# Destination one-hots one chunk later, and sums on three and four blocks of 32 TensorE columns, in a three-layer GCN behind an equivariant message layer

## The chip, the cores and the metric

The kernel runs on one core of a Trainium2 chip. The metric is the device time of one execution in microseconds (us). Of the kernel before, three executions took 5819.27, 5819.81 and 5830.06 us; the median is 5819.81.

## What is computed

There are 12500 nodes with 32 features and 200000 edges, sorted by destination. After a layer norm, a first part (layer 0) sends tensor-product messages along the edges. After a second layer norm come three graph convolutions with self loops and symmetric normalisation. They are what this change touches:

```
norm = deg_inv_sqrt[src] * deg_inv_sqrt[dst]
def conv(x, W, b):                 # W1: 32x128, W2: 128x128, W3: 128x32
    h = x @ W
    msg = h[src] * norm[:, None]
    return segment_sum(msg, dst) + b
h = relu(conv(x, W1, b1)); h = relu(conv(h, W2, b2)); h = relu(conv(h, W3, b3))
return x + h
```

The kernel sums before it multiplies by W1 and after it multiplies by W3, so the rows that it sums over the edges are 32 wide in layers 1 and 3 and 128 wide in layer 2 (WIDTH = [32, 32, 128, 32]).

## The kernel before

**Accumulator.** accT in SBUF holds features on partitions and nodes on the free axis: 12544 columns of nodes and 128 of margin. In layers 1 and 3 it uses partitions 0 to 31 (w = 32), in layer 2 all 128. Partition 32 holds the root of the degree in layer 1, to carry the bias as a 33rd row in the product with W1 (line 1764).

**Two ways over the edges.** Since the edges are sorted by destination, a stretch of edges falls into a narrow window of nodes. The first part of them is done in *groups* of 1024 edges: SP loads the source indices (line 490), POOL gathers the rows of the sources from a table in HBM with 8 indirect DMAs into `rows`, which has 4 buffers (line 641), ACT makes a one-hot of the destinations (lines 699 and 705), TensorE sums the group in `gathered_sum` with 8 fp32 products, rows by one-hot, into `sums` (line 1717; two matmul instructions for each product), and VectorE adds the window of 128 nodes to accT (line 1410, semaphore `added`). POOL may reuse a buffer of `rows` when the group four before has been added.

The rest is done in *buckets* of 1280 edges without a gather: `places` holds for each bucket which source row sits where. A bucket is cut into 5 *chunks*. For a chunk, `mark_sources` makes a one-hot of the sources (VectorE line 1298 in layers 2 and 3, ACT lines 796 and 805 in layer 1), `take` picks the rows from a table in SBUF with 20 products on four blocks of 32 TensorE columns (line 1648), ACT copies the result (`copy_bucket`, line 818), `mark_destinations` makes the one-hot of the destinations (VectorE, line 1313), and `give` sums over them with 5 products into psT or psX by turns (line 1662). After 5 chunks VectorE adds the bucket to accT (`add_bucket`, line 1373). The one-hots and the taken rows are double buffered by chunk.

Layer 1 has 120 groups and 61 buckets, layer 2 has 108 and 71, layer 3 has 80 and 93. Each layer is a loop; a pass has 4, 12 and 8 groups and 2, 8 and 10 buckets. Layer 1 also ranks the edges of later buckets (VectorE lines 1235 to 1280).

**Order.** The order on each engine is written by hand. For chunk k TensorE does `take(k)`, then a group's sum if one falls there, then `give(k - 1)`. VectorE does

```
mark_sources(n, step, k + 1)           # n > 1
...                                    # the group's add, if one falls on k
mark_destinations(n, step, k + 1)      # waits for give(k - 1)
if k % NCK == 0: add_bucket(...)       # the bucket that ended with chunk k - 1
```

In front of layer 3, in `table_after_second`, accT is multiplied by W2 and then by W3 (lines 1777 and 1785); POOL's gathers then start when the new table lies in HBM. At the end TensorE turns accT into blocks of nodes (line 1812), VectorE finishes each of 7 blocks with three instructions (lines 1484 to 1487), and SP stores them.

Of the kernel before, what the change touches and what calls it, by code (L numbers as in the profile page):

```python
# [70 lines left out]
KB = 25  # L71
KC = 5
# [36 lines left out]
def gnn_kernel(nc, x, src, dst, edge_attr, edge_weight, w1, b1, w2, b2,  # L109
               W1, B1, W2, B2, W3, B3, out):  # L110
    ctx = ExitStack()
    with ctx:
# [121 lines left out]
        W1s = sb("W1s", [F + 1, HID])  # L234
# [215 lines left out]
        def _(sp):  # L450
# [134 lines left out]
            sp.dma_start(accT[F:F + 1, 0:NPAD], accT[MUL:MUL + 1, 0:NPAD]).then_inc(counts_moved, 16)  # L585
# [20 lines left out]
        def _(pool):  # L606
# [20 lines left out]
            def gathers(n):  # L627
                def body(step, first, last):
# [15 lines left out]
                    if n == 0 and first:  # L644
# [19 lines left out]
        def _(act):  # L664
# [7 lines left out]
            act.dma_start(W1s[F:F + 1, :], B1.rearrange("(a n) -> a n", a=1)).then_inc(convs_in, 16)  # L672
# [77 lines left out]
            def own_term(n, rows_):  # L750

                for c, at, w in chunks:
# [11 lines left out]
            nc.scalar.activation(accT[F:F + 1, 0:NPAD], accT[F:F + 1, 0:NPAD], ACT.Sqrt,  # L764
                                 bias=one[F:F + 1, :]).then_inc(row_rooted, 1)
# [116 lines left out]
            act.wait_ge(convs_in, 96)  # L882
# [12 lines left out]
        def _(dve):  # L895
# [301 lines left out]
            def prepare_buckets():  # L1197
# [8 lines left out]
                                     iota[:, 0:BJ].unsqueeze(1).to_broadcast([P, BJ, BJ]), ALU.is_gt))  # L1206
                dve.wait_ge(start_b_moved, 32)
# [156 lines left out]
            def add_bucket(n, step, v_, u):  # L1364

                w = WIDTH[n]
# [6 lines left out]
                v.tensor_tensor(accT[0:w, window], accT[0:w, window], (psX if v_ % 2 else psT)[0:w, 0:BWIN],  # L1373
                                ALU.add).then_inc(bucket_added, 1)

            def conv(n):
                w = WIDTH[n]
# [13 lines left out]
                def body(step, first, last):  # L1391
                    groups, chunks_, starts_at = shape(n, last)
                    u = -1
                    for k in range(chunks_):
                        more = not (last and k == chunks_ - 1)
                        if more and n > 1:
                            mark_sources(n, step, k + 1)
                        if k in starts_at:
# [7 lines left out]
                            v_done = (k - 1) // NCK - 1  # L1406
# [18 lines left out]
                mark_destinations(n, Step(dve, 0, n), 0)  # L1425
# [53 lines left out]
            dve.wait_ge(convs_in, 96)  # L1479
# [356 lines left out]
```

## Time and profile before

| | |
|---|---|
| median of three executions | 5819.81 us |
| the profiled execution: its time, and its span | 5822.97 us, 5820.7 us |
| layer 0, and what follows it | 0 to 2280, to 2340 us |
| layer 1, and the product with W1 | 2340 to 3567, to 3626 us |
| layer 2, and the products with W2 and W3 | 3626 to 4739, to 4849 us |
| layer 3, and the output | 4849 to 5803, to 5821 us |
| TensorE, VectorE, ACT, POOL busy | 87%, 73%, 59%, 67% of the span |

The profile is of one execution. Engines are PE (TensorE; PEld is its weight loads), DVE (VectorE), ACT (ScalarE), POOL (GpSimd) and SP. A fp32 product shows as two matmul instructions. The last block of layer 0 is turned at 2288 us.

### The profile page before, as it was taken

How to read it: one execution, taken by the hardware profiler on the slowest of the kernel's cores; microseconds unless marked ns; L12 is line 12 of the kernel's file. 1: busy time of each engine (PE TensorE's matmuls, PEld its weight loads, DVE VectorE, ACT ScalarE, POOL GpSimd, SP SyncE). 2: the span in 40 equal slices, each digit the busy share in tenths (PEclk: the TensorE clock that was granted, in tenths of full speed). 3: DMA queues.
4: the chain of work that ended last, by engine and by line, in shares of the span. 5: the costliest groups of instructions: out<-in, count | busy, mean ns of one | idle time of the engine just before them, and what ended most of it. 6: DMA issues, size and time to landing. Idle time of an engine off the chain costs nothing.

```text
span 5820.7 us, 188939 instructions
## 1 busy us (share of the span) xinstructions
PE 5063.7 (87%) x70625; PEld 3798.9 (65%) x70626; DVE 4230.4 (73%) x8656; ACT 3414.6 (59%) x7724; POOL 3925.4 (67%) x4051
## 2 busy tenths in 40 slices
PE   2999999999999998576766678999999998888887
PEld 1555555555555554566656667988888977777777
DVE  5999999999999998677777775444444434665655
ACT  3666666666666664777777775555555534444434
POOL 4777777777777772677777774777777735665655
PEclk9999999999999999889898888999999988999999
DMA  5111111111111113111111112333333332222222
GB/s 68 39 36 36 36 36 37 36 36 36 36 36 37 36 36 35 34 34 36 34 34 34 35 35 74 83 81 80 81 83 80 79 91 46 56 58 54 58 52 53
DMA packets 474532, 290.23 MB, mean 50 GB/s; under 512 B 264732, under 2 KB 446784, under 8 KB 473393
## 3 DMA queue, kind: packets, MB, share of 16 engines
q0 software_dynamic: 129024, 108.79, 10.0%
q1 hardware_dynamic: 224524, 73.86, 6.3%
q10 hardware_dynamic: 120356, 98.86, 5.7%
q8 instruction: 437, 7.16, 0.5%
q14 instruction: 191, 1.56, 0.1%
HBM read 267.86 MB, written 13.27 MB: 48 GB/s over the span
## 4 chain that ended last, share of the span: by engine, by line
DVE 34%; PE 31%; POOL 16%; issue 15%; DVEq 2%; SPq 1%; DMA 1%; ACT 0%; POOLq 0%; ACTq 0%
POOL rows L641 16%; PE radial L1648 10%; DVE scratch L1086 9%; DVE scratch L1078 8%; DVE scratch L1096 8%; PE sums L1717 6%; PE psT L1662 6%; PE psX L1662 6%; DVE shared L1298 2%; DVE shared L1101 2%; DVE scratch L1110 2%; DVE shared L1057 1%; PE radial L1777 1%; PE radial L1764 1%; DVEq L1371 1%
## 5 line engine op out<-in xcount | busy, mean ns | idle before, releaser
L641 POOL DMA_INDIRECT rows<-table,idx x4032 | 3909.7, 970 | 1869.4 <-issue 1206.5
L699 ACT ACTIVATE dist<-iota,rel 128x128 f32<-128x128 f32 x4032 | 1263.8, 391 | 869.7 <-PE sums L1546 805.4
L1546 PE MATMUL sums<-scratch,onehot 128*128 128x393 f32 x3136 | 1122.1, 500 | 52.2 <-DVE scratch L1110 48.6
L1535 PE MATMUL radial<-w2n,shared 65*128 65x384 f32 x3136 | 1081.4, 488 | 98.6 <-ACT shared L722 98.6
L1546 PEld LDWEIGHTS sums<-scratch,onehot 128*128 128x128 f32 x3136 | 579.5, 190 | 554.6 <-issue 99.0
L1717 PE MATMUL sums<-onehot,rows 128*32 128x128 f32 (+1 forms) x4928 | 710.4, 306 | 242.5 <-DMA rows<-table,idx 228.0
L1535 PEld LDWEIGHTS radial<-w2n,shared 65*128 65x128 f32 x3136 | 581.9, 191 | 511.8 <-ACT shared L722 98.3
L1717 PEld LDWEIGHTS sums<-onehot,rows 128*32 128x32 f32 (+1 forms) x4928 | 598.6, 152 | 310.5 <-issue 200.2
L1086 DVE TENSOR_TENSOR scratch<-radial,shared 128x768 f32<-128x768 f32 x784 | 738.6, 942 | 0.0
L818 ACT COPY scratch<-radial 128x160 f32<-128x160 f32 x770 | 220.9, 287 | 756.7 <-PE radial L1648 754.5
L1313 DVE TENSOR_TENSOR shared<-radial,shared 128x480 f32<-128x480 f32 x770 | 502.2, 654 | 204.0 <-PE psT L1662 97.9
L1662 PE MATMUL psT<-shared,scratch 128*32 128x96 f32 (+1 forms) x5700 | 639.8, 260 | 0.0
L1662 PE MATMUL psX<-shared,scratch 128*32 128x96 f32 (+1 forms) x5550 | 624.7, 261 | 2.0 <-issue 1.3
L1648 PE MATMUL radial<-scratch,shared 128*32 128x32 f32 x30800 | 496.8, 202 | 126.2 <-issue 79.5
L705 ACT ACTIVATE onehot<-dist,one 128x1024 f32<-128x1024 f32 x504 | 580.0, 1151 | 13.1 <-issue 4.3
L1662 PEld LDWEIGHTS psT<-shared,scratch 128*32 128x32 f32 (+1 forms) x5700 | 547.6, 137 | 32.8 <-issue 28.0
L1410 DVE TENSOR_TENSOR accT<-accT,sums 32x128 f32 (+1 forms) x308 | 85.6, 278 | 650.6 <-PE sums L1717 650.4
L1662 PEld LDWEIGHTS psX<-shared,scratch 128*32 128x32 f32 (+1 forms) x5550 | 539.4, 138 | 28.3 <-issue 23.5
L1078 DVE TENSOR_TENSOR scratch<-radial,shared 128x512 f32<-128x512 f32 x784 | 531.0, 677 | 8.4 <-PE radial L1535 2.9
L1298 DVE TENSOR_SCALAR shared<-scratch,line 128x640 f32<-128x640 uint8 x820 | 476.3, 581 | 77.8 <-issue 42.0
L1648 PEld LDWEIGHTS radial<-scratch,shared 128*32 128x32 f32 x30800 | 403.7, 112 | 197.7 <-DVE shared L1298 95.3
L1313 DVE TENSOR_TENSOR shared<-iota,shared 128x480 f32<-128x480 f32 x355 | 235.8, 664 | 365.0 <-PE psT L1662 192.6
(168 smaller groups left out, 5300.2 us busy)
## 6 DMA issues: line engine op xcount, KB each, us to landing
scratch<-places_d ACTq DMA_DIRECT2D x225, 400.0 KB
rows<-table,idx POOLq DMA_INDIRECT x4032
shared<-in_edge_weight SPq DMA_DIRECT2D x195, 256.0 KB, 3.6
idx<-in_src SPq DMA_DIRECT2D x503, 4.0 KB
arena<-norm_d ACTq DMA_DIRECT2D x4, 1568.0 KB, 12.6
table<-arena SPq DMA_DIRECT2D x24, 256.0 KB, 2.3
table<-scratch SPq DMA_DIRECT2D x4, 784.0 KB, 8.9
table<-scratch SPq DMA_DIRECT2D x24, 64.0 KB, 1.8
```

The lines of the kernel that those rows point to most:

```text
L641: (pool.indirect_dma_start(rows[:, r, j, 0:WIDTH[n]], None, tables[n], bass.IndirectOffsetOnAxis(ap=idx[:, r, j:j + 1], axis=0)) .then_inc ...
L699: ins = nc.scalar.activation(dist[:, j, :], iota[:, :], ACT.Abs, scale=-1.0, bias=rel[:, bass.ds(step.tile(u) + j, 1)])
L705: nc.scalar.activation(onehot[:, u % 2, :, :], dist[:, :, :], ACT.Relu, scale=-1.0, bias=one[:, :]).then_inc(onehot_ready[u % 2], 1)
L1078: prod = v.tensor_tensor(prodA[:, h, t:t + 2, :].rearrange("p t (m s) -> p t m s", s=16), R[:, :, 0:256].rearrange("p t (m s) -> p t m s", ...
L1086: last = v.tensor_tensor(msg[:, h, t:t + 2, 17:401].rearrange("p t (i u s) -> p t i (u s)", i=3, u=MUL), R[:, :, 256:384].unsqueeze(2).to_ ...
L1298: v.tensor_scalar(from_src[:, k % 2, :, :, :], places[:, v_ % 2, :, c * KC * CAP:(c + 1) * KC * CAP].rearrange("p i (t r) -> p i t r", r=CAP),
L1313: v.tensor_tensor(to_dst[:, k % 2, :, :], numbers.unsqueeze(1).to_broadcast([P, KC, BWIN]), at.unsqueeze(2).to_broadcast([P, KC, BWIN]), A ...
L1535: last = nc.tensor.matmul(radial[q % 2][:, k, 0:RDIM], hidT[:, u % 2, 2 * q + k, :], w2n[:, :], start=True, stop=True)
L1546: last = nc.tensor.matmul(sums[:, u % 2, 0:SEGW], onehot[:, u % 2, 4 * h + k, :], msg[:, h, k, MUL:MUL + SEGW], start=(h == 0 and k == 0), ...
L1648: last = nc.tensor.matmul(d, from_src[:, h, i, t, :], table_of(n, s), start=True, stop=True, tile_position=(0, 32 * i))
L1662: last = nc.tensor.matmul((psX if v % 2 else psT)[0:w, 0:BWIN], taken[:, h, t, 0:w], to_dst[:, h, t, :], start=(c == 0 and t == 0), stop=( ...
L1717: mm = nc.tensor.matmul(sums[0:w, u % 2, 0:WIN], rows[0:used, r, j, 0:w], onehot[0:used, u % 2, j, :], start=(j == 0), stop=(j == TPG - 1))
```

## The change

- VectorE's `mark_destinations(k)` is issued in chunk k, directly behind `mark_sources(k + 1)` and before the group's add, where before it issued that of chunk k + 1 behind the add. It waits for `give(k - 2)`. `add_bucket` comes one chunk later. This holds for all three layers.
- In layers 1 and 3 the products of a group's sum and of `give` go by turns to 3 and 4 blocks of 32 columns (`PARTS`), and so to 96 and 128 partitions of PSUM. VectorE adds all of them to 96 and 128 partitions of accT, which holds partial sums.
- The partial sums are added by the next product: W1 is loaded three times on 96 partitions, the bias row moves to partition 96; at the output the 98 transposes become products with `fold`, a 128x32 matrix that also adds the four parts.
- POOL clears partitions 32 to 63 of accT before layer 1, and 32 to 63 and 64 to 127 before layer 3, once the last product with W2 has been made. VectorE waits for this before its first chunk of the layer.

```diff
+PARTS = [1, 3, 1, 4]
+BIAS = 3 * F
...
+                if n == 1:
+                    pool.wait_ge(blocks_turned, NTB)
+                    nc.gpsimd.memset(accT[F:2 * F, :], 0.0).then_inc(acc_cleared, 1)
+                elif n == 3:
+                    pool.wait_ge(weighed[1], NCH)
+                    nc.gpsimd.memset(accT[F:2 * F, :], 0.0).then_inc(acc_cleared, 1)
+                    nc.gpsimd.memset(accT[2 * F:4 * F, :], 0.0).then_inc(acc_cleared, 1)
                 if n < 2:
                     pool.wait_ge(table_out[n], 32)
...
-            act.dma_start(W1s[0:F, :], W1).then_inc(convs_in, 16)
+            for part in range(PARTS[1]):
+                act.dma_start(W1s[part * F:(part + 1) * F, :], W1).then_inc(convs_in, 16)
...
+                link(v.tensor_reduce(fold[:, :], ident[:, :].rearrange("p (a f) -> p f a", f=F), X, ALU.add))
...
                         if more and n > 1:
                             mark_sources(n, step, k + 1)
+                        mark_destinations(n, step, k)
                         if k in starts_at:
...
-                            v_done = (k - 1) // NCK - 1
+                            v_done = (k - 7) // NCK
...
-                            v.tensor_tensor(accT[0:w, window], accT[0:w, window], sums[0:w, u % 2, 0:WIN],
+                            v.tensor_tensor(accT[0:rows_, window], accT[0:rows_, window], sums[0:rows_, u % 2, 0:WIN],
                                             ALU.add).then_inc(added[u % UNROLL], 1)
-                        if more:
-                            mark_destinations(n, step, k + 1)
-                        if k % NCK == 0 and not (first and k == 0):
-                            add_bucket(n, step, k // NCK - 1, u)
+                        if k % NCK == 1 and not (first and k == 1):
+                            add_bucket(n, step, (k - 1) // NCK - 1, u)
...
                 for t in range(KC):
-                    last = nc.tensor.matmul((psX if v % 2 else psT)[0:w, 0:BWIN], taken[:, h, t, 0:w],
-                                            to_dst[:, h, t, :], start=(c == 0 and t == 0),
-                                            stop=(c == NCK - 1 and t == KC - 1))
+                    part = (c * KC + t) % PARTS[n]
+                    last = nc.tensor.matmul((psX if v % 2 else psT)[part * F:part * F + w, 0:BWIN], taken[:, h, t, 0:w],
+                                            to_dst[:, h, t, :], start=(c * KC + t < PARTS[n]),
+                                            stop=(c * KC + t >= KB - PARTS[n]), tile_position=(0, part * F))
...
                     for j in range(TPG):
-                        mm = nc.tensor.matmul(sums[0:w, u % 2, 0:WIN], rows[0:used, r, j, 0:w],
-                                              onehot[0:used, u % 2, j, :], start=(j == 0), stop=(j == TPG - 1))
+                        part = j % PARTS[n]
+                        mm = nc.tensor.matmul(sums[part * F:part * F + w, u % 2, 0:WIN], rows[0:used, r, j, 0:w],
+                                              onehot[0:used, u % 2, j, :], start=(j < PARTS[n]), stop=(j >= TPG - PARTS[n]),
+                                              tile_position=(0, part * F))
...
-                    last = nc.tensor.transpose(radial[0][:, k % 2, j * F:(j + 1) * F],
-                                               accT[0:F, at:at + P], ident[0:F, 0:F])
+                    last = nc.tensor.matmul(radial[0][:, k % 2, j * F:(j + 1) * F],
+                                            accT[:, at:at + P], fold[:, :], start=True, stop=True)
```

## Rows read from the trace of the kernel before

**Rows 1.** Windows: us, busy us (instructions) by engine, PEclk, DMA share, GB/s.

```profile
2340.00:3567.00 1227.00, 842.17 (x19172) 751.04 (x19172) 890.71 (x2125) 927.72 (x1986) 912.64 (x960) 0.89 0.17 34
3626.00:4739.00 1113.00, 1096.16 (x19478) 990.27 (x19478) 464.83 (x888) 635.44 (x1681) 827.11 (x852) 0.99 0.31 80
...
4750.00:4830.00 80.00, 79.22 (x238) 56.30 (x238) 20.68 (x47) 17.72 (x25) 0.00 (x0) 0.50 0.23 65
4849.00:5803.00 954.00, 802.69 (x24530) 727.64 (x24530) 574.32 (x1103) 410.29 (x1188) 614.20 (x629) 0.96 0.24 55
5806.00:5818.00 12.00, 8.49 (x70) 7.82 (x70) 11.10 (x19) 0.00 (x0) 0.00 (x0) 0.50 0.74 117
```

**Rows 2.** Groups by line, POOL, layers 1, 2 and 3: busy, mean; idle, releasers.

```profile
L641 POOL DMA_INDIRECT rows<-table,idx x960 | 912.6, 951 | 401.4 <-issue 292.3 <-DMA idx<-in_src 109.1
...
L641 POOL DMA_INDIRECT rows<-table,idx x864 | 838.4, 970 | 331.0 <-issue 258.4 <-DMA idx<-in_src 63.9 <-DVE accT L1410 8.7
...
L641 POOL DMA_INDIRECT rows<-table,idx x640 | 625.0, 977 | 454.0 <-issue 190.2 <-DVE accT L1410 145.5 <-DMA idx<-in_src 118.2
```

**Rows 3.** Waits in layer 3 (4849 to 5803): us in total, times, longest.

```profile
DVE accT L1410 <- PE sums L1717: 174.6, 80, 8.6
POOL rows L641 <- DVE accT L1410: 145.5, 48, 10.2
...
DVE shared L1313 <- PE psT L1662: 81.7, 126, 2.9
...
DVE shared L1313 <- PE psX L1662: 57.2, 132, 1.3
```

**Rows 4.** Groups by line and form, TensorE, layer 3.

```profile
L1662 PE MATMUL psT<-shared,scratch 128*32 128x96 f32 x2350 | 236.7, 248 | 0.0
...
L1717 PE MATMUL sums<-onehot,rows 128*32 128x128 f32 x1280 | 168.9, 290 | 23.1 <-DMA rows<-table,idx 10.2 <-issue 10.1 <-ACT onehot L705 2.7
```

**Rows 5.** Timeline at a loop end of layer 3: start, us, instruction, idle before.

```profile
5145.03 0.55 DVE L1298 TENSOR_SCALAR shared<-scratch,line 128x640 f32<-128x640 uint8 x1 [3.42 <-issue]
5146.84 0.44 PE L1648 MATMUL radial<-scratch,shared 128*32 128x32 f32 x16 [2.64 <-issue]
...
5151.23 0.28 DVE L1410 TENSOR_TENSOR accT<-accT,sums 32x128 f32 x1 [5.64 <-PE sums L1717]
```

**Rows 6.** Timeline, TensorE, layer 2.

```profile
4210.04 1.30 PE L1648 MATMUL radial<-arena,shared 128*32 128x128 f32 x40
4211.32 2.02 PE L1717 MATMUL sums<-onehot,rows 128*128 128x128 f32 x16
```

**Rows 7.** Timeline at the end: last gather, last group, output.

```profile
5794.69 0.95 POOL L641 DMA_INDIRECT rows<-table,idx  x1 [0.30 <-issue]
...
5797.21 1.93 PE L1717 MATMUL sums<-onehot,rows 128*32 128x128 f32 x16 [3.14 <-DMA rows<-table,idx]
...
5810.10 1.70 PE L1812 MATMUL radial<-ident,accT 32*128 32x32 f32 x14 [0.18 <-DVE scratch L1487]
...
5816.88 0.63 DVE L1487 SCALAR_TENSOR_TENSOR scratch<-scratch,xn 128x448 f32<-128x448 f32 x1
```

**Rows 8.** Timeline, TensorE, layer 3, from a `give` to a `take`.

```profile
5102.48 0.82 PE L1662 MATMUL psX<-shared,scratch 128*32 128x96 f32 x8
5103.07 0.26 PE L1648 MATMUL radial<-scratch,shared 128*32 128x32 f32 x6
5103.14 0.25 PE L1662 MATMUL psX<-shared,scratch 128*32 128x96 f32 x1
```

**Rows 9.** Timeline: the clearing in layer 0, starts of layers 1 and 3.

```profile
123.27 10.68 POOL L646 MEMSET accT<- 128x12672 f32 x1
...
2342.24 0.94 POOL L641 DMA_INDIRECT rows<-table,idx  x1 [109.14 <-DMA idx<-in_src]
...
4827.61 1.20 PE L1777 MATMUL radial<-accT,W2s 128*128 128x256 f32 x2
4828.60 2.61 PE L1785 MATMUL sums<-W3s,rows 128*128 128x32 f32 x12
...
4834.80 0.94 POOL L641 DMA_INDIRECT rows<-table,idx  x1 [118.22 <-DMA idx<-in_src]
```

More of the change, by code:

```diff
@@ L233, in gnn_kernel @@
         w2n = sb("w2n", [HID0 + 1, RDIM])
-        W1s = sb("W1s", [F + 1, HID])
+        W1s = sb("W1s", [BIAS + 1, HID])
+        fold = sb("fold", [P, F])
         W2s = sb("W2s", [HID, HID])
@@ L584, in _ @@
             sp.wait_ge(blocks_turned, NTB)
-            sp.dma_start(accT[F:F + 1, 0:NPAD], accT[MUL:MUL + 1, 0:NPAD]).then_inc(counts_moved, 16)
+            sp.dma_start(accT[BIAS:BIAS + 1, 0:NPAD], accT[MUL:MUL + 1, 0:NPAD]).then_inc(counts_moved, 16)
             sp.wait_ge(start_b_made, 1)
@@ L668, in _ @@
             act.dma_start(w2raw[HID0:HID0 + 1, :], b2.rearrange("(a n) -> a n", a=1)).then_inc(consts_in, 16)
-            act.dma_start(W1s[0:F, :], W1).then_inc(convs_in, 16)
+            for part in range(PARTS[1]):
+                act.dma_start(W1s[part * F:(part + 1) * F, :], W1).then_inc(convs_in, 16)
             act.dma_start(W2s[:, :], W2).then_inc(convs_in, 16)
             act.dma_start(W3s[:, :], W3).then_inc(convs_in, 16)
-            act.dma_start(W1s[F:F + 1, :], B1.rearrange("(a n) -> a n", a=1)).then_inc(convs_in, 16)
+            act.dma_start(W1s[BIAS:BIAS + 1, :], B1.rearrange("(a n) -> a n", a=1)).then_inc(convs_in, 16)
             act.dma_start(B2c[:, :], B2.rearrange("(n a) -> n a", a=1)).then_inc(convs_in, 16)
@@ L762, in _ @@
             act.dma_start(norm_d, norm_cols[:, :]).then_inc(norm_out, 16)
-            nc.scalar.activation(accT[F:F + 1, 0:NPAD], accT[F:F + 1, 0:NPAD], ACT.Sqrt,
-                                 bias=one[F:F + 1, :]).then_inc(row_rooted, 1)
+            nc.scalar.activation(accT[BIAS:BIAS + 1, 0:NPAD], accT[BIAS:BIAS + 1, 0:NPAD], ACT.Sqrt,
+                                 bias=one[BIAS:BIAS + 1, :]).then_inc(row_rooted, 1)
             def set_iotas(n):
@@ L1364, in add_bucket @@
             def add_bucket(n, step, v_, u):
-                w = WIDTH[n]
+                rows_ = PARTS[n] * WIDTH[n]
                 dve.wait_ge(bucket_summed, chunk_count(n, step, v_ * NCK + NCK - 1))
@@ L1372, in add_bucket @@
                 window = bass.ds(start, BWIN)
-                v.tensor_tensor(accT[0:w, window], accT[0:w, window], (psX if v_ % 2 else psT)[0:w, 0:BWIN],
+                v.tensor_tensor(accT[0:rows_, window], accT[0:rows_, window], (psX if v_ % 2 else psT)[0:rows_, 0:BWIN],
                                 ALU.add).then_inc(bucket_added, 1)
             def conv(n):
-                w = WIDTH[n]
+                rows_ = PARTS[n] * WIDTH[n]
                 def ranking(step, k, last):
@@ L1476, in _ @@
             conv(3)
-            dve.wait_ge(convs_in, 96)
+            dve.wait_ge(convs_in, 128)
             for k in range(NTB):
@@ L1764, in table_after_first @@
                         last = nc.tensor.matmul(radial[0][:, c % 2, j * P:(j + 1) * P],
-                                                accT[0:F + 1, at + j * P:at + (j + 1) * P], W1s[:, :],
+                                                accT[0:BIAS + 1, at + j * P:at + (j + 1) * P], W1s[:, :],
                                                 start=True, stop=True)
@@ L1800, in _ @@
             conv(1)
-            pe.wait_ge(convs_in, 96)
+            pe.wait_ge(convs_in, 128)
             table_after_first()
```

4 lines of the change are left out of this document (2 added, 2 removed).

## The prediction

> **What bounds the kernel now.** I read the stretches first: busy time of each engine in each stage and the granted clock [rows 1]. The reader is to see that the two changed layers are not alike. Then, for each layer of the GCN, what POOL's gathers waited for [rows 2], because POOL is the one engine that can only work 4 groups ahead of `added`; then who waits for whom in layer 3 [rows 3], and the forms of the sums [rows 4].
>
> Layer 1 (2340 to 3567 us) is paced by POOL. Its 960 gathers take 912.6 us and, apart from the one wait at the start, sit idle only for issue, 292.3 us: 1204.9 us in all, of 1227 [rows 2]. No gather waits for `added`. VectorE is busy 891 us and TensorE 842 us [rows 1]. A cheaper sum on TensorE is hidden there.
>
> Layer 2 (3626 to 4739) is TensorE's: busy 1096 of 1113 us [rows 1], and POOL (838.4 + 258.4) is almost as long; only 8.7 us of its idle time is for `added` [rows 2]. Its width is 128, so PARTS is 1 and only VectorE's order changes.
>
> Layer 3 (4849 to 5803) is neither. TensorE is busy 803 of 954 us, VectorE 574, ACT 410, POOL 614 [rows 1]. Gathers need 625.0 + 190.2 = 815.2 us by themselves, and wait another 145.5 us for `added` [rows 2]. VectorE waits 174.6 us for the group's sum, and 81.7 + 57.2 us at the destination one-hot for the `give` of the chunk before [rows 3]; TensorE waits in turn for VectorE's source one-hot, which stands behind that destination one-hot in the queue. So layer 3 is a ring of TensorE and VectorE. Its rest is at the loop's end: VectorE stands 3.42 us and TensorE 2.64 us with nothing released by anyone, and the next group's add starts only at 5151.23, 6.2 us behind the source one-hot ahead of it [rows 5].
>
> **The change, part by part, against the profiled span of 5820.7 us.**
>
> *Sums on 4 blocks.* A chunk's `give` is 10 matmuls in some 1.0 us (236.7 us for the 235 chunks whose sum is in psT, [rows 4]; psX is alike); one lasts 0.248 us, so the pitch is (0.98 - 0.25) / 9 = 0.082 us. Do different column blocks run side by side? The trace has this: `take` puts 40 matmuls of 128 moving columns on four blocks in 1.30 us, (1.30 - 0.28) / 39 = 0.026 us apart, while 16 of the same width on one block take 2.02 us, 0.116 apart [rows 6]. That is four at a time. I take full overlap. Five products on four blocks leave one block two, which is 4 instructions: 0.25 + 3 x 0.082 = 0.50 us; saved 0.48 a chunk, 465 x 0.48 = 223 us of TensorE. A group's sum goes from 1.93 us [rows 7] to 0.27 + 3 x 0.11 = 0.60: 80 x 1.33 = 106 us. TensorE's 803 us become about 475. The other bound is no overlap at all: 803 stay, and only the order helps.
> The Trainium skill, "TensorE: Matmul & The Clock Gate", Part 3, says that matmuls start in strict program order; both halves of an fp32 product being on one block, only about half the overlap would be left. The trace disagrees: six matmuls of `take` start at 5103.07, before the last of the `give` ahead of them at 5103.14 [rows 8]. By the page a `give` would be 0.6 us and a group sum 1.1, TensorE would need about 560 us, and the total would be the same.
>
> *Destination one-hot one chunk later.* It then waits for the `give` before last, and stands behind one source one-hot, not ahead of it. The 138.9 us of waits at L1313 go, and so does TensorE's wait behind them. Nothing new is queued behind it but the group's add, which waits for the group's sum anyway. VectorE without these waits: 954 - 174.6 - 138.9 = 640 us [rows 3], issue time and the wait at the layer's start included. That is 8.0 us a group, and POOL's 815.2 / 80 is 10.2. ACT is busy 410 us [rows 1], 5.1 a group. So POOL sets layer 3's pace. The loop's end costs the chain 6 to 9 us once in 8 groups, and the rows have 4 buffers (40 us of gathers), so this is covered; were that cover gone, nine such ends would cost up to 80 us.
> In layer 2 TensorE's 17 idle us are all there is to gain; each `give` still has its one-hot a `take` (1.30 us) ahead. I take 0, bounds -10 and +10.
>
> *POOL's clearing.* A memset of accT's 12672 columns is 10.68 us on 128 partitions [rows 9]; fewer partitions should not be cheaper (bounds 2.7, by the share of partitions, and 10.7 each). Layer 1's one runs after the last block is turned (2288), in the shadow of the layer norm and of the first two rankings; the first gather there is at 2342.24 [rows 9]. I take 0; if it kept VectorE off memory all the while, 10.7. Layer 3's two start at the end of the last product with W2, 4827.61 + 1.20 = 4828.8 [rows 9], and end at 4850.3. The first gather is now at 4834.80 [rows 9] and moves by 15.5 us. As POOL sets the pace, all of it counts.
>
> Gathers then run from 4850.3 for 815.2 us. I add 8 us, because 93 bucket loads are squeezed into less time and some gathers will queue: the last ends at 5673.5. Now it ends at 5794.69 + 0.95 = 5795.6 [rows 7]. **Layer 3: -122.1 us**, and -2 for the last sum and the `give`s behind it. Layer 1's end, behind its last gather, is VectorE's ranking chain and a few `give`s: -1.5.
>
> *Output.* 98 transposes, one instruction each, become fp32 products, two each. Fourteen take 1.70 us at granted clock 0.50 [rows 1, 7], hidden by VectorE's three steps per block: 0.62 + 0.62 + 0.63. A product with 128 stationary and 32 moving columns at clock 0.50 is (2.61 - 0.40) / 11 = 0.20 us per instruction [rows 9], so a block of 28 is 5.6 us and now above VectorE's 1.9. Seven blocks: 39.2 + 1.9, less 2 us as the first runs before the clock falls, so 39.1, against 14.3 us now (5803.2 to 5816.88 + 0.63, [rows 7]): **+25**. Will the clock rise under this work? The projection with W3, TensorE 79.22 of 80 us busy, stayed at 0.50 (1.2 GHz) [rows 1]. If it did rise to 2.4 GHz, at the 0.116 us of [rows 6] per instruction, +11.
>
> *Small.* `fold` is one short reduction on VectorE: +0.3. W1s's two more loads and the weights of 97 rows: 0, at the start ACT waits for x, and a product's time goes by its columns. Adds of 96 or 128 partitions instead of 32: under 0.02 us each, 0.
>
> Sum: -122.1 - 2 - 1.5 + 0.3 + 25 = -100.3, 5720.4 for the span. The profiled execution took 5822.97 in all, the three runs' median is 5819.81; I take the difference off the median: **5719.5 us**.
>
> **Rivals.**
> *A, the forecast*: POOL sets layer 3. Speaks for it: it ran its first gathers there unhindered, and layer 1 shows POOL pacing a busier VectorE. Own range 5695 to 5745: clock at the output (-14), gathers queued (+25), layer 2 (+-10).
> *B, the ring stays, slower clock.* TensorE, now waiting for rows, spends more time at 1.2 GHz, as in layer 1 (0.89), ACT's one-hots for the groups stand in front of its copies, and the loop's ends are not absorbed. Half of layer 3's 122 us is lost, at 11.0 us a group instead of 10.3: +61, 5780. Against it: 8.0 against 10.2 us a group.
> *C, slower.* The costs at both ends, 15.5 + 25 = 40 us, are sure, the gain hangs on layer 3's pace. It is 11.9 us a group now; if it stays above 11.4, the kernel is slower; at an unchanged pace 5860. It needs blocks that do not overlap at 96 and 128 columns and a drain at each switch between `take` and `give`. The overlap [rows 6] and the missing gap [rows 8] speak against both.
> *D, no change in effect*: gain and costs cancel, layer 3 at 11.4 us a group.
>
> **How the numbers follow.** A 0.72, B 0.16, C 0.08, D 0.04. The time is A's. Range: A's and most of B's, 5692 to 5788. A measurement here can tell 0.2%, 12 us. Faster by more: A, B, 0.88; same 0.04; slower 0.08.
>
> **What would show it.** Layer 3's first gather near 4850, no gather waiting for `added`, 10.2 to 10.4 us a group; VectorE waiting for the group's sum, and TensorE for rows; `give` near 0.5 us and the group's sum near 0.6 at full clock; L1313 hardly waiting; layers 1 and 2 within 10 us; 196 instructions at the output over some 39 us. I am wrong if gathers still wait for `added`, if the memsets are far from 10.7 us, or if layer 2 moves.

## The result and the profile after

The changed kernel takes 5783.9 us (median of 4 runs, 5778.1 to 5789.2), the kernel before 5821.4 beside it: a ratio of 0.9939, 95% interval 0.9926 to 0.9951. It is faster, by 37 us and not by the 100 forecast. The profiled execution has a span of 5787.1 us against 5820.7.

The same stretches as in [rows 1]: layers 1, 2 and 3, and the output (window; then us busy and, in brackets, instructions of PE, PEld, DVE, ACT and POOL; granted clock, DMA share, GB/s).

```profile
2340.00:3567.00 1227.00, 665.48 (x19117) 556.95 (x19120) 904.75 (x2136) 933.36 (x1996) 911.63 (x960) 0.67 0.17 34
3626.00:4730.00 1104.00, 1088.40 (x19331) 983.21 (x19331) 479.32 (x882) 626.26 (x1660) 820.86 (x847) 0.99 0.31 81
4837.00:5737.00 900.00, 521.80 (x24522) 460.73 (x24526) 561.99 (x1101) 404.42 (x1185) 620.41 (x641) 0.83 0.24 58
5740.00:5783.90 43.90, 41.91 (x196) 41.77 (x196) 13.12 (x21) 0.00 (x0) 0.00 (x0) 0.50 0.20 32
```

TensorE's work in layer 3 did shrink as the diff promises, from 803 to 522 us. The stretch did not follow: 900 us are left, in which no engine is busy 70% of the time. POOL's gathers of layer 3 come first (against [rows 2]; shortest, median and longest in ns, first and last start in us, then POOL's idle time ahead of them). Then who waits between 4860 and 5760 (against [rows 3]; us in total, times, longest):

```profile
L645 POOL DMA_INDIRECT rows<-table,idx x640: 938/944/1287, 4837.7 to 5733.4; - x160
  issue: 190.4, 603
  DVE accT L1424: 86.4, 36
```

```profile
ACT scratch L830 <- PE radial L1660: 432.9, 356, 6.0
PEld radial L1660 <- issue: 283.6, 175, 4.0
PE radial L1660 <- issue: 262.5, 168, 3.8
...
DVE accT L1424 <- PE sums L1731: 155.0, 73, 7.8
DVE shared L1311 <- PE radial L1660: 134.7, 141, 2.4
POOL rows L645 <- DVE accT L1424: 86.4, 36, 8.3
...
PE radial L1660 <- DVE shared L1311: 35.4, 31, 2.0
...
DVE shared L1326 <- PE psT L1675: 14.8, 19, 1.7
...
DVE shared L1326 <- PE psX L1675: 6.3, 10, 1.3
```

VectorE's wait at the destination one-hot (L1326) is down from 139 us to 21, nearly gone, as forecast. But it comes back one instruction earlier: the source one-hot (L1311) now waits 134.7 us for TensorE's `take`. TensorE's own wait for that source one-hot, which was to go too, is still 35.4 us (33.2 before, between 4860 and 5790). Gathers still wait for `added`, and ACT waits for `take`. Most of TensorE's idle time is put down to "issue", 262.5 us in 168 pieces: it stands still and the profile shows nothing that it waits for. The timeline shows where (start, duration, and in brackets the idle time ahead):

```profile
5162.26 0.55 PE L1660 MATMUL radial<-scratch,shared 128*32 128x32 f32 x39 [2.10 <-issue]
5162.65 0.49 PE L1675 MATMUL psX<-shared,scratch 128*32 128x96 f32 x10
...
5164.06 0.45 PE L1660 MATMUL radial<-scratch,shared 128*32 128x32 f32 x26
5166.31 0.33 PE L1660 MATMUL radial<-scratch,shared 128*32 128x32 f32 x14 [1.79 <-issue]
```

A `take` stops after the 26th of its 40 matmuls and goes on 1.79 us later, in the middle of an operation, where no semaphore stands. The view of the DMA queues has what comes at these moments: queue 8, kind "instruction", 16,384 B a packet. First layer 1 (2360 to 3560), then layer 2 (3620 to 4700), then layer 3 (4850 to 5740); the columns are packets, MB and share.

```profile
q8 instruction: 17, 0.28, 0.1%
q8 instruction: 177, 2.90, 1.1%
q8 instruction: 220, 3.60, 1.7%
```

I read these packets as the code of TensorE. Layer 1, whose loop is short, has 17 of them in 1200 us. In layers 2 and 3 they come through the whole layer: a packet per 6.1 us in layer 2, per 4.05 us in layer 3. Call it a pause when two matmuls start more than 0.6 us apart. Layer 3 has 228 pauses (4860 to 5730), 402 us in all, almost one for each packet. From a packet's end to the end of the next pause it is 1.27 to 1.59 us (10th to 90th percentile of some 220 packets). The kernel before has 109 pauses (4860 to 5790), 136 us in all, and the 90th percentile of the same distance is 15.9 us: half of its packets have no pause of their own, because, as I read it, TensorE's slower work covered the fetching.

### The profile page after: what moved, and what is told of

Its sections match the earlier page's. It is cut to its first block, busy times and chain, and to the rows that moved or that the text cites. A ratio compares the mean times of both kernels' runs of the same rounds, so it can differ in the third digit from the quotient of the medians.

```text
span 5787.1 us, 189184 instructions
## 1 busy us (share of the span) xinstructions
PE 4623.7 (80%) x70723; PEld 3356.7 (58%) x70724; DVE 4254.0 (74%) x8657; ACT 3407.2 (59%) x7724; POOL 3948.6 (68%) x4054
## 4 chain that ended last, share of the span: by engine, by line
DVE 33%; PE 30%; issue 18%; POOL 17%; DVEq 1%; SPq 1%; DMA 1%; ACT 0%; POOLq 0%; ACTq 0%
POOL rows L645 16%; PE radial L1660 12%; DVE scratch L1098 9%; DVE scratch L1090 8%; DVE scratch L1108 8%; PE psT L1675 5%; PE psX L1675 5%; PE sums L1731 5%; DVE shared L1113 2%; DVE scratch L1122 2%; DVE shared L1069 1%; PE radial L1792 1%; PE radial L1827 1%; DVE shared L1311 1%; PE sums L1800 1%
## 5 line engine op out<-in xcount | busy, mean ns | idle before, releaser
L1660 PE MATMUL radial<-scratch,shared 128*32 128x32 f32 x30800 | 610.2, 218 | 309.9 <-issue 263.2
L1731 PE MATMUL sums<-onehot,rows 128*32 128x128 f32 (+1 forms) x4928 | 463.1, 341 | 482.6 <-DMA rows<-table,idx 459.7
L1660 PEld LDWEIGHTS radial<-scratch,shared 128*32 128x32 f32 x30800 | 519.3, 127 | 363.2 <-issue 290.4
L1311 DVE TENSOR_SCALAR shared<-scratch,line 128x640 f32<-128x640 uint8 x820 | 484.4, 591 | 281.5 <-PE radial L1660 221.5
L1731 PEld LDWEIGHTS sums<-onehot,rows 128*32 128x32 f32 (+1 forms) x4928 | 354.4, 162 | 533.4 <-issue 296.1
L1424 DVE TENSOR_TENSOR accT<-accT,sums 128x128 f32 (+1 forms) x308 | 87.9, 286 | 653.6 <-PE sums L1731 649.1
L1675 PE MATMUL psT<-shared,scratch 128*32 128x96 f32 (+1 forms) x5700 | 519.1, 299 | 28.8 <-issue 16.4
L1675 PE MATMUL psX<-shared,scratch 128*32 128x96 f32 (+1 forms) x5550 | 507.1, 297 | 37.7 <-DVE shared L1326 27.8
L1326 DVE TENSOR_TENSOR shared<-radial,shared 128x480 f32<-128x480 f32 x770 | 497.9, 650 | 47.3 <-PE psT L1675 23.4
L1660 PE MATMUL radial<-arena,shared 128*32 128x128 f32 x14200 | 463.4, 276 | 14.5 <-DVE shared L1311 10.7
L1108 DVE TENSOR_REDUCE scratch<-scratch 128x64 f32<-128x1024 f32 x392 | 473.9, 1209 | 0.0
L1675 PEld LDWEIGHTS psT<-shared,scratch 128*32 128x32 f32 (+1 forms) x5700 | 399.5, 152 | 72.7 <-issue 54.0
```

Source lines behind the costliest of these rows:

```text
L1108: v.tensor_reduce(msg[:, h, :, 0:16], prodA[:, h, :, :].rearrange("p t (m s) -> p t m s", s=16), X, ALU.add).then_inc(scalars_ready[h], 1)
L1311: v.tensor_scalar(from_src[:, k % 2, :, :, :], places[:, v_ % 2, :, c * KC * CAP:(c + 1) * KC * CAP].rearrange("p i (t r) -> p i t r", r=CAP),
L1660: last = nc.tensor.matmul(d, from_src[:, h, i, t, :], table_of(n, s), start=True, stop=True, tile_position=(0, 32 * i))
L1675: last = nc.tensor.matmul((psX if v % 2 else psT)[part * F:part * F + w, 0:BWIN], taken[:, h, t, 0:w], to_dst[:, h, t, :], start=(c * KC + ...
L1731: mm = nc.tensor.matmul(sums[part * F:part * F + w, u % 2, 0:WIN], rows[0:used, r, j, 0:w], onehot[0:used, u % 2, j, :], start=(j < PARTS[ ...
```

## The experiments

**The theories.** *S, supply*: TensorE gets a packet of instructions per 3.8 to 4.0 us at best. A packet holds some 256 instructions. That is an estimate: in the straight code at the end of h4, below, 19,382 matmuls and weight loads run in 78 packets, 248 a packet, and waits come on top. So a chunk of some 100 instructions costs 1.6 us whatever each does, and column blocks, which leave their number as it is, bring little. *T*: TensorE's execution counts, and the blocks' halving of it is the gain. *V*: the chain of VectorE and ACT through a chunk sets the pace. *P*: POOL sets more of it than it seems.

**Layer 3 without its gathers.** Leaving out layer 3's gathers and index loads (the sums take whatever rows lie in the buffers) takes POOL away:

```
-                    pe.wait_ge(gathered[r], rows_gathered(step, n, u, 1))
+                    if n < 3:
+                        pe.wait_ge(gathered[r], rows_gathered(step, n, u, 1))
...
-                sweep(pool, body, n)
+                if n < 3:
+                    sweep(pool, body, n)
```

h1 is the changed kernel in this form:

> The changed kernel with layer 3's gathers and the loads of their indices left out (the groups' sums take whatever rows lie there, so the output is not the reference's). On the chips of the earlier runs TensorE issued 3 or 4 instructions per 0.7 us while POOL issued gathers; without gathers layer 3 is free of that on any chip, and POOL can't set its pace. The time from the first to the last sum of a group of layer 3: theory S (instruction supply, 256 instructions per 4.0 us) about 835 us, 89.5 us a pass of 50 chunks and 8 groups, with a stall of TensorE behind each 16 KB packet. Rival P (POOL's gathers set more of the pace than thought): well below 800 us. Rivals V and T agree with S on this kernel alone.

h2 the kernel before with VectorE's new order alone:

> VectorE's new order alone (one column block), with layer 3's gathers left out as in the first kernel. Theory S: TensorE executes as many instructions, so the time is 89.5 us a pass too, or a little more where a chunk's own work (1.73 us by layer 3's 803 busy us over 465 chunks) comes near the supply: 835 to 870 us for the layer's sums. Rival T (the blocks halved TensorE's work, and that gave the gain): 900 us or more.

h3 leaves out one product in five:

```
-                for t in range(KC):
+                for t in range(KC - (n == 3)):
```

> The changed kernel without layer 3's gathers, and with the last 4 of the 20 products of a take left out in layer 3: 16 of some 107 instructions a chunk. VectorE's and ACT's work per chunk is unchanged. Theory S: 16 x 15.7 ns = 0.25 us less a chunk, 77 us a pass, 720 us for the layer's sums; packets 4.0 us apart as before. Rival V (VectorE's and ACT's chain of a chunk sets the pace): 835 us as in the first kernel, packets 4.7 us apart. Rival T (TensorE's own work): 8 matmuls x 25 ns a chunk less, 745 us, but with no stall tied to packets.

h4 cuts the loop, so that its code is as short as layer 1's:

```
-LOOP = [(UNROLL, 0), (4, 2), (12, 8), (8, 10)]
-REST = [(UNROLL, 0), (4, 3), (12, 7), (8, 3)]
+LOOP = [(UNROLL, 0), (4, 2), (12, 8), (4, 2)]
+REST = [(UNROLL, 0), (4, 3), (12, 7), (4, 55)]
```

> The changed kernel without layer 3's gathers, and with layer 3's loop cut to 4 groups and 2 buckets (some 1,200 TensorE instructions, as many as layer 1's loop, which fetched no packets), rest 4 groups and 55 buckets. No instruction's work changes. Theory S: no packets in the loop, no stalls of 1.8 us; a pass of 10 chunks and 4 groups takes 14 to 17 us in place of the 19.6 us that supply would need (10 x 1.68 + 4 x 0.7); in the rest, 275 chunks at 1.68 us or so, 465 us. Rivals V and T: 19.6 us a pass with or without packets.

The groups' adds of layer 3: in the changed kernel, then in h1, h2, h3 and h4 (first and last start). Each is a single execution; the kernel before took 5827.8 us on that chip.

```profile
L1424 DVE TENSOR_TENSOR accT<-accT,sums x80: 286/289/293, 4850.3 to 5737.0; 128x128 f32 x80
```

```profile
L1425 DVE TENSOR_TENSOR accT<-accT,sums x80: 286/289/291, 4843.0 to 5712.0; 128x128 f32 x80
```

```profile
L1412 DVE TENSOR_TENSOR accT<-accT,sums x80: 274/276/278, 4861.7 to 5752.3; 32x128 f32 x80
```

```profile
L1425 DVE TENSOR_TENSOR accT<-accT,sums x80: 272/289/291, 4839.8 to 5575.9; 128x128 f32 x80
```

```profile
L1425 DVE TENSOR_TENSOR accT<-accT,sums x80: 274/289/291, 4840.6 to 5474.0; 128x128 f32 x80
```

The work inside 4950 to 5550, for h1, h2 and h3:

```profile
4950.00:5550.00 600.00, 340.32 (x16612) 301.46 (x16615) 369.37 (x746) 261.90 (x768) 0.00 (x0) 0.83 0.17 48
```

```profile
4950.00:5550.00 600.00, 505.68 (x16244) 484.15 (x16243) 370.78 (x731) 255.15 (x751) 0.00 (x0) 0.95 0.17 46
```

```profile
4950.00:5550.00 600.00, 359.99 (x16750) 309.37 (x16751) 428.90 (x886) 306.30 (x917) 0.00 (x0) 0.87 0.19 57
```

And their instruction packets in the same 600 us:

```profile
q8 instruction: 151, 2.47, 1.7%
```

```profile
q8 instruction: 147, 2.41, 1.7%
```

```profile
q8 instruction: 157, 2.57, 1.9%
```

What is to be seen:
- *P falls.* Without a single gather, layer 3's adds span 869.0 us against 886.7. Between 4950 and 5550 ACT's copies, one a chunk, come every 1.90 us in both, so a pass of 50 chunks and 8 groups takes 95.0 us against 95.2. POOL's share is 17.7 us, 16 of them behind the last full pass, where 8 groups meet only 3 buckets. (I had expected 835, from 89.5 us a pass; it is 95.)
- *T falls.* One column block (h2) has TensorE busy 506 of 600 us, four (h1) 340, and yet 16,244 matmuls get through against 16,612, 147 packets against 151. The layer takes 890.6 us against 869.0: blocks that take a third off TensorE's busy time give 2.4%. Both my numbers missed (S 835 to 870, T 900 or more); the ratio is what S says.
- *V falls.* h3 takes nothing from VectorE or ACT, only 16 TensorE instructions of some 100 a chunk, and a chunk's copy by ACT comes every 1.60 us in place of 1.90; the layer takes 736.0 us in place of 869.0. The stream runs on as fast, 27.9 matmuls per us for 27.7, with as many packets. Sixteen instructions of 256 per 3.9 us are 0.24 of the 0.30 us. The other 0.06 is that the packets come 3.82 us apart in place of 3.97 (600 us over 157 and over 151), at 0.42 packets a chunk; why they do is open.

h4 leaves the least room. Its stretch in the short loop (4860 to 5150) and in the long rest (5170 to 5470), windows first, then packets:

```profile
4860.00:5150.00 290.00, 201.37 (x10121) 175.37 (x10119) 213.75 (x468) 284.83 (x818) 0.00 (x0) 0.96 0.17 50
5170.00:5470.00 300.00, 170.37 (x9694) 157.88 (x9688) 213.61 (x426) 63.39 (x212) 0.00 (x0) 0.89 0.19 56
```

```profile
q8 instruction: 4, 0.07, 0.1%
q8 instruction: 78, 1.28, 1.9%
```

In the short loop packets cease: 4 in 290 us. A pass of 10 chunks and 4 groups takes 16.0 us. By h4's rest a chunk costs 1.55 us (its copies are that far apart, and few groups lie there), and by h1 a group costs (95.0 - 50 x 1.55) / 8 = 2.2, its share of the loop's end included, so with fetching the same pass would be some 24 us. That is an estimate; counted by instructions alone, with some 40 for a group (0.6 us), it would be 18. The 16.0 us are below both. Without the fetching the next bound shows: ACT, busy 284.8 of 290 us. In the rest packets come every 3.85 us again. S holds.

One thing more can be read from these rows. In the loop of h1 a packet carries 33,227 / 151 = 220 matmuls and weight loads, in the straight rest of h4 248. So about a tenth of what is fetched in the loop is not run; the loop's end is where I would look for it, but no run here separates it.

**The complete kernels on other chips.** The other runs fell on chips where the kernel before takes 9069 to 9198 us, not 5820. There is one difference that the traces show. In e2, on such a chip, the first window is one in which POOL issues 8 gathers, the second one in which it issues none:

```profile
7817.20:7825.90 8.70, 3.40 (x70) 2.06 (x66) 2.13 (x4) 1.19 (x2) 6.57 (x8) 0.50 0.09 13
7829.00:7836.00 7.00, 6.34 (x266) 5.02 (x258) 5.83 (x12) 3.28 (x12) 0.00 (x0) 0.65 0.21 64
```

8 matmuls per us beside gathers, 38 without. In this place weight loads come in ones to fours, 0.7 to 1.4 us apart, from 2.3 us after the first gather starts until 1.8 us after the last one ends. On the chips of the kernel before and after nothing of this is in the trace. I don't know its cause. I read it so that these runs are another experiment: time there is close to gathers plus TensorE's work, one after the other.

The order alone (four times; the edits are those of the diff's VectorE part) and the blocks alone (three times):

> The kernel before with VectorE's new order alone: sums on one column block, no clearing, transposes at the output. Theory S (supply): in layer 3 of the changed kernel TensorE stands still about 1.8 us once in about 4.0 us, each time just behind a 16 KB packet of its instruction queue (218 packets, 256 instructions each, 3.98 us apart), so a stream of 256 instructions can't take less than 4.0 us there, and the column blocks bring little, since they leave the number of instructions as it is. Layer 3's gathers would span 900 to 930 us (896 in the changed kernel, 960 before); layer 1's end and the output are as before (W1's product 40 us, output 14 us): 5755 to 5790 us in all. Rival T (TensorE's execution is what counts, and the blocks halved it): layer 3 stays near the kernel before, 950 us or more, 5805 to 5820 us in all.

> The changed kernel with VectorE's old order: column blocks, clearing, and products at the output stay. Theory S: blocks shorten a give but not the supply; VectorE's old order adds its waits, so layer 3's gathers span 920 to 950 us, and the costs of the blocks (output +29, clearing 21 and 6) stay: 5810 to 5840 us. Rival T: the blocks are where layer 3's gain comes from: span near 896 to 905 us, 5785 to 5795 us in all.

> The kernel before with VectorE's new order alone, again, as the runs of the first four kernels were on a chip where the kernel before took 9166 us and waited in all its layers for things that the trace does not show. The expectations are those of the first: theory S (instruction supply) 5755 to 5790 us, layer 3's gathers 900 to 930 us; rival T (the blocks halved TensorE's work, and that is the gain) 5805 to 5820 us, layer 3's gathers 950 us or more.

> The changed kernel with VectorE's old order, again, for the same reason. Theory S: layer 3's gathers span 920 to 950 us, 5810 to 5840 us in all. Rival T: 896 to 905 us, 5785 to 5795 us in all.

> VectorE's new order alone, once more, to see it on a chip where the kernel before takes 5820 us; on the two chips so far (9166 and 9069 us for the kernel before) TensorE's products stood 0.6 us apart for stretches of 10 to 15 us at a time, and the order was worth 0 to 0.4%. On a chip without that: theory S (instruction supply) 5755 to 5790 us, layer 3's gathers 900 to 930 us; rival T (the blocks halved TensorE's work, and that is the gain) 5805 to 5820 us, 950 us or more. If the chip is of the slow kind again, the ratio is 0.996 to 1.002.

> VectorE's new order alone, complete, on a chip like that of the kernels without layer 3's gathers (5828 us for the kernel before). There, without gathers, its layer 3 took 890.6 us from the first to the last group's add (the changed kernel 869.0), 97 us a pass against 95. With the gathers the last 8 groups wait for POOL (some 16 us). Supply (S): layer 3's adds span 905 to 915 us, the whole 5785 to 5800 us, so the order alone brings most of what the whole change does. Rival T (the blocks bring it): 5810 us or more.

> The changed kernel with VectorE's old order, complete. S: TensorE then waits for VectorE at each chunk as in the kernel before, but its give is 0.5 us shorter, so a pass takes 96 to 101 us (95.5 with the new order, 102 before): 5790 to 5830 us in all. Rival T: as the changed kernel, 5780 to 5788 us.

| kernel | this, us | ratio to before on the same chip |
|---|---|---|
| order alone, e1 | 9187.8 | 1.0017 (0.9997 to 1.0037) |
| order alone, f1 | 9050.8 | 0.9964 (0.9941 to 0.9987) |
| order alone, g1 | 9195.6 | 1.0000 (0.9984 to 1.0016) |
| order alone, j1 | 9056.3 | 0.9983 (0.9955 to 1.0011) |
| blocks alone, e2 | 8874.3 | 0.9682 (0.9652 to 0.9712) |
| blocks alone, f2 | 8757.2 | 0.9655 (0.9605 to 0.9706) |
| blocks alone, j2 | 8768.8 | 0.9648 (0.9628 to 0.9669) |

On these chips blocks bring 3.2 to 3.5% and the order 0 to 0.4%. None of the expected times in us applies. That fits T: where gathers hold TensorE up, what it executes in the remaining time counts. No run takes the gathers out on such a chip, so this is argued and not shown. What the table shows is that on these chips the blocks are worth more than the order.

> The changed kernel with layer 3's 80 groups and 93 buckets shared out evenly: a loop of 12 groups and 14 buckets and a rest of 20 and 23, in place of 8 and 10 and a rest of 8 and 3. No instruction more or less is executed but for loop ends. Theory S: each chunk with its share of the group costs 1.79 us of instruction supply (89.5 us a pass of 50 chunks) and the last 8 groups with 3 buckets wait for POOL; evenly shared, 465 chunks take 832 us in place of 896: 5720 to 5735 us in all. Rival V (VectorE's and ACT's chain sets 10.2 to 11.2 us a group whatever the share of buckets): 5775 us or more.

> The changed kernel with a shorter loop in layer 3: 4 groups and 6 buckets (some 3,400 TensorE instructions a pass, in place of 5,700), rest 32 groups and 21 buckets. In layer 1, whose loop has some 1,300, only 15 packets of instructions were fetched in 1,200 us, one layer's first pass, loop and rest. Theory S: if 3,400 instructions are held on the chip, packets cease in the loop, the stalls of 1.8 us with them, and POOL sets the pace, 40.8 us a pass: layer 3 near 820 us, 5700 to 5715 in all. If they are not held, packets go on every 4.0 us, a pass takes 53 us, and with the uneven share it is 5845 to 5870 us. Rivals T and V: a pass of 30 chunks takes 53 us with no packets at all, if the loop is held; stalls as before.

> VectorE's new order without blocks, and layer 3's groups and buckets shared out evenly (loop 12 and 14, rest 20 and 23, in place of 8 and 10, rest 8 and 3). Theory S: a chunk with its share of a group costs 1.79 us (or up to 1.86 where TensorE's own work is the longer), 465 of them 832 to 865 us; with neither clearing nor products at the output 5700 to 5730 us. Rival V (VectorE's and ACT's chain sets the time by group, not by chunk): no gain from the even share, as without it.

> The changed kernel, with the last 4 of the 20 products of each take left out in layer 3 (the output is then not the reference's): 16 of some 107 TensorE instructions a chunk less; VectorE's, ACT's and POOL's work is unchanged. Theory S: supply 1.54 us a chunk, so a pass of 50 chunks would need 77 us and POOL's 81.6 us sets it: layer 3's gathers 820 to 835 us in place of 896, packets 4.2 us apart or more, few gathers waiting; 5705 to 5725 us in all. Rival V (VectorE's and ACT's chain): layer 3 unchanged, 890 us or more, 5775 us or more.

e3 took 8907.5 us (0.9712, 0.9677 to 0.9747), e4 8976.7 (0.9796, 0.9766 to 0.9826), f3 9012.1 (0.9929, 0.9902 to 0.9955), f4 8763.6 (0.9648, 0.9610 to 0.9685). The changed kernel itself was not run on such a chip, so for e3, e4 and f4 there is nothing to set them against: inconclusive. f3 against f1, on one chip (9012.1 against 9050.8), says that the even share is worth some 0.4% there, with intervals that touch. One thing e4 does show: its loop of 4 groups and 6 buckets still fetched 164 packets in its 12 passes (7438 to 8424). Code of that length, some 3,400 TensorE instructions, is not held; that of h4's 4 and 2, some 1,200, is.

**Taking the costs back.** j3 keeps the blocks in layer 1 alone: layer 3 sums on one block, its two clearings go, and the output is turned by transposes as before.

```
-PARTS = [1, 3, 1, 4]
+PARTS = [1, 3, 1, 1]
...
-                    last = nc.tensor.matmul(radial[0][:, k % 2, j * F:(j + 1) * F],
-                                            accT[:, at:at + P], fold[:, :], start=True, stop=True)
+                    last = nc.tensor.transpose(radial[0][:, k % 2, j * F:(j + 1) * F],
+                                               accT[0:F, at:at + P], ident[0:F, 0:F])
```

> The changed kernel with column blocks in layer 1 alone: layer 3's sums on one block, no clearing before layer 3, transposes at the output as before. S: layer 3 loses 21 us (890.6 for 869.0 in the runs without gathers), the output gains 29, the start of layer 3 some 5 to 12; W1's product, which took 26 us on 97 rows and 40 on 33, stays at 26: 5765 to 5780 us. If the rows of W1s are not what makes that product faster, 5780 to 5795.

j4 and k1 also keep E0 at 80 groups and set

```
-GATHERED = [NG, 120, 108, 80]
-LOOP = [(UNROLL, 0), (4, 2), (12, 8), (8, 10)]
-REST = [(UNROLL, 0), (4, 3), (12, 7), (8, 3)]
+GATHERED = [NG, 120, 108, 84]
+LOOP = [(UNROLL, 0), (4, 2), (12, 8), (28, 30)]
+REST = [(UNROLL, 0), (4, 3), (12, 7), (28, 30)]
```

> The third kernel of this call, with layer 3's edges shared as 84 groups and 90 buckets in place of 80 and 93, in three equal parts of 28 and 30 (a loop of one pass, no rest of another share). S: supply needs 90 x 9.1 + 84 x 0.7 = 880 us, POOL 84 x 10.2 = 857, and no stretch waits for POOL's last groups: 25 us less than the third kernel, 5740 to 5757 us. Rival (gathers and supply disturb each other at equal load): no gain.

> Column blocks in layer 1 alone, VectorE's new order, and layer 3's edges as 84 groups and 90 buckets in three equal parts, once more, to see it on a chip where the kernel before takes 5820 us (on the chip of the last four kernels it took 9078, and this one 8961). S, where gathers do not hold TensorE up: 5740 to 5757 us, a pass of 28 groups and 30 buckets 290 to 295 us, POOL's gathers 286 of them; W1's product 26 us, output 14 us. Rival (equal load of POOL and supply leaves each waiting for the other): no better than the changed kernel, 5775 us or more.

j3 took 9004.7 us (0.9910, 0.9888 to 0.9932), j4 8961.4 (0.9864, 0.9822 to 0.9906), k1 8995.7 in its one run. All were on chips of the second kind, where the blocks alone are better than any of them. That j4 beats the changed kernel on a chip of the first kind stays an estimate. The output and the product with W1s can be read on any chip, since no gathers run beside them. The product with W1s, in j1 (33 rows) and in j3 (97 rows):

```profile
5066.00:5106.00 40.00, 39.75 (x195) 39.70 (x196) 16.23 (x25) 0.00 (x0) 0.00 (x0) 0.53 0.53 156
```

```profile
4998.50:5025.00 26.50, 26.48 (x196) 25.66 (x196) 16.17 (x24) 0.00 (x0) 0.00 (x0) 0.88 0.80 228
```

The same 196 matmuls of 128 columns, TensorE busy throughout in both: with 33 rows the granted clock is 0.53 (1.2 GHz nearly all the time), with 97 it is 0.88 (2.4 GHz for most of it), and the product takes 40 us or 26. So it is in every kernel here: 40 to 41 us in the seven with 33 rows, 25 to 27 us in the thirteen with 97. But the rows are not alone in this: the kernels with 97 rows all have blocks in layer 1 as well, and their TensorE had less to do before the product (busy 510 of the 1000 us ahead of it in j3, at clock 0.54, against 588 at 0.70 in j1). No run separates the two. The output, from its first matmul to its last, is 12.7 us in j3 and 41.6 in j2.

## Why the forecast was right in sign and wrong in size

The forecast's terms against the profiled execution, in us:

| step | forecast | measured |
|---|---|---|
| layer 1, and POOL's clearing ahead of it | -1.5 | +5.0 |
| product with W1s | 0 | -13.5 |
| layer 2 and the products behind it | 0 (-10 to +10) | -4.1 |
| clearing ahead of layer 3, less the 6 us that its first gather came late anyway | +15.5 | +15.6 |
| layer 3, first gather to the end of the last | -137.6 | -64.2 |
| last sum and gives | -2 | -2.1 |
| output | +25 | +29.7 |

The table splits the forecast's 122.1 us at layer 3's first gather (15.5 - 137.6); its +0.3 for `fold` is left out. The measured column sums to the -33.6 of the spans.

**The step that failed** is "So POOL sets layer 3's pace". The sum under it took 8.0 us of VectorE a group and 475 us of TensorE in the layer against POOL's 10.2 us a group, and these were near enough: the `give` is 0.49 us at full clock (forecast 0.50), the group's sum 0.64 (0.60), TensorE's busy time 522 us. By the rule that I had weighed (the Trainium skill, "TensorE: Matmul & The Clock Gate", Part 3) they would be 0.6 and 1.1; the trace stays with the rows. What was missing is a resource: TensorE's instruction stream. A pass of 8 groups and 50 chunks takes 95 us, 11.9 us a group, with gathers or without (h1), with one block or four to within 2.2 us (h2), shorter as soon as there are fewer instructions (h3), and the limit goes when the loop is short (h4). It could have been read before. Instruction packets between 4950 and 5550, in the kernel before and in the changed one:

```profile
q8 instruction: 144, 2.36, 1.6%
```

```profile
q8 instruction: 151, 2.47, 1.7%
```

That is one per 4.17 us against one per 3.97, only 5% apart, and TensorE already stood "issue" for 79.5 us in layer 3 of the kernel before. About half of this, 41 us, was at seven loop ends. I took that standing [rows 5] for a cost that comes once in 8 groups and is covered; the other half, spread through the passes, I passed over.

The time of 5783.9 us lies inside the stated range of 5692 to 5788, but only in the part that was there for rival B; A's own range ended at 5745.

**Which part gave the gain.** Without gathers, the blocks on top of the order shorten layer 3 by 21.6 us (890.6 to 869.0) and the whole by 12.5 (h2's span of 5774.4 to h1's 5761.9), their costs and the product with W1s included. That product alone is 14.5 us shorter in h1 (26.2 against 40.7), so without this gain, which was not planned, the blocks would bring about nothing on this kind of chip. Of the 55.9 us by which layer 3's adds drew together in the complete kernel (942.6 to 886.7), that would leave some 34 to the order, if the blocks are worth the same with gathers as without. This is an estimate from single runs, and the order alone was not timed complete on such a chip.

**Rival B** said 5780, close to what came, but that is luck. Its mechanism is not what the runs show: the clock did fall, from 0.96 to 0.83, but h2 at 0.95 is slower than h1 at 0.83. The clock fell together with TensorE's busy share, and did not set the time. B was nearest where it doubted that the loop's ends are absorbed. **C and D** needed blocks that don't overlap; they overlap.

**The clearings.** Their price was right and does not depend on the partitions. The one before layer 1 and VectorE's work beside it, then the two before layer 3:

```profile
2289.30 10.65 POOL L656 MEMSET accT<- 32x12672 f32 x1 [55.37 <-PE radial L1607]
...
2291.42 3.42 DVE L929 TENSOR_REDUCE mu<-xn 128x98 f32<-128x3136 f32 x1
2294.87 5.14 DVE L930 TENSOR_SCALAR mu<-mu 128x98 f32<-128x98 f32 x1
...
4816.22 10.65 POOL L659 MEMSET accT<- 32x12672 f32 x1 [111.47 <-PE radial L1792]
...
4826.92 10.66 POOL L660 MEMSET accT<- 64x12672 f32 x1
```

The first was costed at 0, bound 10.7, and cost 6: a tensor_scalar of 98 elements, 0.21 us in the kernel before, ends with the memset after 5.14, and layer 1's first gather comes at 2348.4 for 2342.2. The reduction ahead of it took 3.42 us beside the memset, as in the kernel before. The Trainium skill, "SBUF — State Buffer", section "SBUF: two separate sides", has the shared pair of ports as an exclusive lock, which a one-input VectorE instruction wants only in its two-port modes. The trace agrees as far as it goes: one of the two one-input instructions waits to the memset's end and the other doesn't, but it doesn't show their modes. The two before layer 3 delay its first gather as forecast, but as POOL doesn't set the pace, what counts is the first add: it comes 34.1 us behind the end of the product with W2 (4816.2), where it used to come 27.9 us behind it (4828.8), so some 6 of the 15.5 us are felt.

**Output.** The mechanism was right, 196 instructions at granted clock 0.50 that nothing hides, the size a little low: VectorE gets a block every 5.97 us, 0.213 us an instruction for the 0.20 taken, and the first block had no faster clock.

```profile
5775.98 0.62 DVE L1496 TENSOR_TENSOR scratch<-radial,dis 128x448 f32<-128x448 f32 x1 [4.03 <-PE radial L1827]
...
5781.95 0.62 DVE L1496 TENSOR_TENSOR scratch<-radial,dis 128x448 f32<-128x448 f32 x1 [4.03 <-PE radial L1827]
```

**The product with W1s.** "A product's time goes by its columns" missed 13.5 us in the kernel's favour, more than a third of the 37 us gained. The number of instructions and their columns stayed; the clock that is granted changed, from 0.54 before (3567 to 3607) to 0.89 (3572 to 3599). The forecast had taken the time at an unchanged clock without a reason. The Trainium skill, "TensorE: Matmul & The Clock Gate", "Step-by-step: what each phase is for", says of the load of the weights that the number of rows doesn't matter there; no run here says otherwise. Whether it was the rows that changed the clock, or layer 1's lighter work ahead of the product, is open.

## What to carry to other kernels

Count the instructions of a loop body beside its work: where the queue of kind "instruction" brings packets at a steady pace and an engine's idle time is "issue" in the middle of an operation, suspect that the engine waits for its code; here fewer instructions (h3) and a body short enough to be held (h4) helped, and cheaper instructions hardly did. Before pricing a gain as "the next engine sets the pace", take that engine out in a run: one run of the layer without gathers would have shown that POOL doesn't set it. Small matmuls that run side by side cut an engine's busy time, which is not the same as time.

## What the runs showed of the hardware that I had not expected

- TensorE's code comes in packets of 16,384 B, 3.8 to 4.0 us apart at best (157 in 600 us in h3, 151 in h1), and after a pause TensorE goes on 1.3 to 1.6 us behind a packet's end. A loop with 4 groups and 2 buckets is held (4 packets in 290 us), one with 4 and 6 is not (164 packets in 12 passes).
- The granted clock of the product with W1s, which keeps TensorE busy all the time, was 0.52 to 0.54 in the kernels with 33 rows and 0.88 to 0.93 in those with 97 rows, which also have blocks in layer 1. At the output, with 128 rows and 32 moving columns, it stayed at 0.50 for 42 us.
- A memset by POOL of 12,672 columns takes 10.65 us on 32 partitions, 10.66 on 64, 10.68 on 128.
- On four chips the kernel before takes 9.1 to 9.2 ms in place of 5.8. TensorE is slow there while POOL issues gathers: 8 matmuls per us against 38 in e2's two windows. The cause is open.
